# Turning the first half of the heads one hidden tile later in a fused mLSTM and MLP block

## What is computed

```
xn = _layernorm(x, axis=-1)
x = x + _L0_attn_ref(xn, ...) + _L0_ffn_ref(xn, ...)

q = x @ Wq.T; k = x @ Wk.T; v = x @ Wv.T; o_preact = x @ Wog.T
h, state = _mlstm_scan(q, k, v, i_pre, f_pre)
h_norm = _multihead_norm(h, gamma).reshape(B, S, -1)
h_out = jax.nn.sigmoid(o_preact) * h_norm
y = h_out @ Wout.T

gated = jax.nn.silu(gate) * up
return jnp.einsum('bsh,dh->bsd', gated, w_down)
```

## Time and profile before

| | us |
|---|---|
| median of 3 runs | 3110.75 |
| lowest, highest | 3110.28, 3111.6 |
| the profiled execution | 3110.59 |
| its span, first to last instruction | 3108.9 |

### The profile page before, as it was taken

One profiled execution on the slowest core, in us unless ns is written; L12 is line 12 of the kernel. 1 busy time (PEld: TensorE's weight loads), 2 busy tenths in 40 slices (PEclk: granted clock), 3 DMA queues, 4 the chain that ended last, 5 costly groups with the idle time before them and its releaser, 6 DMA issues.

```text
span 3108.9 us, 62468 instructions
## 1 busy us (share of the span) xinstructions
PE 3047.3 (98%) x22090; PEld 2194.9 (71%) x22090; DVE 2347.1 (75%) x5913; ACT 1113.4 (36%) x2160; POOL 781.7 (25%) x1121
## 2 busy tenths in 40 slices
PE   4999999999999999999999999999999999999999
PEld 2677777777777777777777777777777777777776
DVE  7877777777777777777777777777777777777777
ACT  6333333333323333333333333333233333333332
POOL 4222222222222222222222222222222222222222
PEclk9999999999999999999999999999999999999999
DMA  5000000000000000000000000000000000000000
GB/s 224 8 14 13 13 7 7 13 13 13 13 0 13 13 13 13 7 7 13 13 13 13 7 7 13 13 13 13 0 13 13 13 13 7 7 13 13 13 13 7
DMA packets 20334, 51.09 MB, mean 16 GB/s; under 512 B 1506, under 2 KB 1634, under 8 KB 18274
## 3 DMA queue, kind: packets, MB, share of 16 engines
q1 hardware_dynamic: 20322, 50.95, 4.4%
HBM read 34.16 MB, written 16.78 MB: 16 GB/s over the span
## 4 chain that ended last, share of the span: by engine, by line
issue 73%; POOL 22%; PE 2%; DVE 1%; POOLq 1%; ACT 1%; DMA 0%; SPq 0%; DVEq 0%; ACTq 0%
POOL arena L555 9%; POOL pair_r L545 4%; POOL small L574 3%; POOL arena L565 2%; POOL begun L562 1%; POOL small L462 1%; DVE amax L757 1%; PE work L1154 0%; POOLq L554 0%; DMA arena<-w_v_dram 0%; POOL small L464 0%; POOL small L467 0%; POOL small L460 0%; PE work L1119 0%; ACT weights L611 0%
## 5 line engine op out<-in xcount | busy, mean ns | idle before, releaser
L1117 PE MATMUL work<-xt,weights 128*128 128x256 f16 x4608 | 1256.0, 273 | 0.0
L1119 PE MATMUL work<-xt,weights 128*128 128x256 f16 x4608 | 1256.0, 273 | 0.0
L1118 PE MATMUL work<-xt,weights 128*128 128x256 f16 x4608 | 1255.9, 273 | 0.0
L555 POOL TENSOR_TENSOR arena<-arena 128x256 f16<-128x256 f32 x512 | 359.5, 702 | 1628.2 <-ACT arena L689 1628.2
L689 ACT ACTIVATE arena<-arena 128x256 f16<-128x256 f32 x512 | 213.3, 417 | 1057.8 <-DVE arena L983 1057.8
L1117 PEld LDWEIGHTS work<-xt,weights 128*128 128x128 f16 x4608 | 478.5, 104 | 69.2
L1118 PEld LDWEIGHTS work<-xt,weights 128*128 128x128 f16 x4608 | 450.9, 98 | 69.7
L1119 PEld LDWEIGHTS work<-xt,weights 128*128 128x128 f16 x4608 | 450.8, 98 | 52.3
L1117 PE MATMUL acc<-weights,arena 128*128 128x512 f16 x1024 | 388.1, 379 | 0.5 <-POOL arena L555 0.5
L1118 PE MATMUL acc<-weights,arena 128*128 128x512 f16 x1024 | 388.1, 379 | 0.0
L1119 PE MATMUL acc<-weights,arena 128*128 128x512 f16 x1024 | 388.1, 379 | 0.0
(11 more groups left out here) (212 smaller groups left out, 4150.7 us busy)
## 6 DMA issues: line engine op xcount, KB each, us to landing
arena<-x_dram SPq DMA_DIRECT2D x33, 512.0 KB, 3.4
out_dram<-arena SPq DMA_DIRECT2D x32, 512.0 KB, 2.8
weights<-w_g_dram SPq DMA_DIRECT2D x4, 1024.0 KB, 13.2
weights<-w_u_dram SPq DMA_DIRECT2D x4, 1024.0 KB, 20.4
arena<-w_d_dram SPq DMA_DIRECT2D x4, 1024.0 KB, 27.2
arena<-w_qk_dram SPq DMA_DIRECT2D x1, 1024.0 KB, 6.3
arena<-w_v_dram SPq DMA_DIRECT2D x1, 1024.0 KB, 8.3
weights<-w_o_dram SPq DMA_DIRECT2D x1, 1024.0 KB, 25.4
```

Source lines behind the costliest of these rows:

```text
L555: g.tensor_tensor(hh[:, j % HB, 1, :], tt[:, j % 2, :], hh[:, j % HB, 0, :], ALU.subtract).then_inc(h_ready, 1)
L1117: t.matmul(dst, w[0], a[0], start=first, stop=False, skip_group_check=True)
L1118: t.matmul(dst, w[0], a[1], start=False, stop=False, skip_group_check=True)
L1119: return t.matmul(dst, w[1], a[0], start=False, stop=last, skip_group_check=True)
```

## The change

In the table AFTER, hoT0 moves from behind tile 11 to behind tile 12, ahead of the other steps there. In USES it changes places with ffn12, to keep the table in PE's order. Since banks go by place, ffn12 now has bank 2 and hoT0 bank 0; all other uses keep their bank.

```diff
 USES = (["gates", "q", "k", "v0", "v1", "ffn0", "ffn1", "ffn2", "ffn3", "wT", "ffn4", "wbc", "ffn5", "o0",
-         "ffn6", "st0", "ffn7", "ffn8", "st1", "ffn9", "ffn10", "st2", "ffn11", "hoT0", "ffn12", "st3", "o1",
+         "ffn6", "st0", "ffn7", "ffn8", "st1", "ffn9", "ffn10", "st2", "ffn11", "ffn12", "hoT0", "st3", "o1",
          "ffn13", "att0", "ffn14", "ffn15", "hoT1", "att1"])
...
-AFTER[11] = ["hoT0", "turn12", "turn13"]
-AFTER[12] = ["pv3", "o1", "center1"]
+AFTER[11] = ["turn12", "turn13"]
+AFTER[12] = ["hoT0", "pv3", "o1", "center1"]
```

## The result

The changed kernel takes 3129.01 us (median, 3127.39 to 3129.73), the kernel before 3111.1 us (3110.28 to 3111.6); the ratio is 1.0057, with a 95% interval of 1.0042 to 1.0072. It is 18 us slower (17.9 between the medians).

What follows compares the result with a forecast made beforehand. PE, busy 98% of the span, was taken as the bound. Removing the 0.42 us wait and adding one of about 1.0 makes o1 0.57 us later a block: 32 x 0.57 = 18.2 on 3110.75 gives 3129 us, range 3123 to 3136.

Steps and rivals of the forecast that it cites:

- The old wait and its price: At hoT0, PE's transposes wait for DVE's line 1078 of heads0, costing 0.42 us a block between starts.
- The new wait: At o1, PE waits 1.02 us for DVE's line 983 to free tile 12's bank, behind eight transposes.
- The delay from DVE's end to PE's start: At o1, PE starts 0.05 us after DVE frees the bank; 0.15 as the other end.
- Sum: Over the loop, 32 x 0.57 = 18.2 us on top of 3110.75, giving 3129.0 us.
- No second wait behind it: Behind o1, tile 13 has 0.98 us of room and att0 finds hoT0's low part ready, so neither waits.
- Transposes and POOL: On DVE behind tile 11's pair, eight transposes beside POOL's line 555 go free, taking 2.65 us.
- The rival of a held transpose: POOL holds DVE's transposes behind tile 11's pair: 0.42 us a block on top, 0.99 in all, 3142 us; chance 0.06.
- the fourth rival: o1 doesn't wait because DVE frees tile 12's bank 1.02 us earlier: 15.1 us won, 3096 us; chance 0.05.
- the 1093.89 given: Latest end of tile 12's last matmul on PE, placed before the transposes (0.44 us) and down(10) (1.30 us).

Runs made afterwards that it cites:

- the first experiment: Changed kernel with turn12 and turn13 moved from behind tile 11 to behind center1 (tile 12) and scale1 (tile 13): 3095.86 us, ratio 0.9953.

## Why the prediction was right

- **The old wait and its price.** Said: 0.42 us a block between starts, set by heads0. The changed kernel has tile 12 right behind down(9), and with nothing else in the way (the first experiment) a block falls from 94.49 to 94.05 us: 0.44, against the 0.45 worked out.
- **The new wait.** Said: o1 waits for tile 12's line 983, behind eight transposes. Shown by the view of waits, and by the runs with none and with half of the transposes. The wait between starts is 1.43 - 0.45 (the distance without a wait, in the first experiment) = 0.98 us in the block shown, where 1.02 was worked out; the blocks of the two kernels differ by 95.07 - 94.05 = 1.02. Line 983 started 3.58 behind the same line of tile 11 (1096.63 to 1100.21), as the sum 0.45 + 3.13 had it.
- **The delay from DVE's end to PE's start.** I took 0.05 from a row ahead of the loop and kept 0.15 as the other end. Measured: 0.06.
- **Sum.** 0.57 a block was forecast, 0.58 measured; 3129.0 against 3129.01. The hundredths are luck: the runs spread over 2.3 us, and the kernel before came out at 3111.1 and not at the 3110.75 that the sum started from.
- **No second wait behind it.** Right: ACT's copy for the heads and line 1084 come in the places worked out, tile 13 and att0 don't wait.
- **Transposes and POOL.** Line 555 runs beside them (1097.58) and the eight take 2.64. The rival of a held transpose is out. DVE instructions with two inputs in SBUF did take longer beside POOL's in the run with turn11 moved.
- **What was wrong.** One remark in the fourth rival, that transposes ahead of tile 11's pair would free the bank in time. That run gave 3160. The slip was to follow DVE's queue alone, without ACT's, in which the tanh of tile 12 stands behind the copy of tile 11. A slip without effect: between tile 12's last matmul and o1 PE also has pv3, 0.9 us (1098.81 to 1099.26 and 0.45 to the next), so tile 12's matmuls end earlier than the 1093.89 given, and the tanh was no limit all the more.
- **What was not seen.** I gave the exchange of banks no part in the gain: with the old bank tile 12 would have waited for st2, drained behind heads0. It had no part in the forecast time, since the change does both. Nor did I see that the old wait may be in part POOL's: line 1078, which ends it, takes 0.95 us beside line 555 and 0.69 without it.

## What to carry to other kernels

When a step is moved past a use of a shared buffer, list for every later use which use it now follows, and place that one's release through the queues of all engines that it passes. Here the step that was waited for had moved out of the way, and the next user of its bank had inherited a neighbour with eight transposes in front. A freed bank is a threshold: four transposes cost nothing and eight cost 33 us, so look for the slack (0.87 us with none of the transposes, 0.34 with four) before moving anything into it. And look at the place to which a step is moved: turn13 behind heads1 cost 0.22 us a block, which the view of PE's waits doesn't list and only the distances between starts show.

## What the runs showed of the hardware that was not expected

- Behind a wait of about 2.24 us of PE, once a block in an otherwise dense stream, TensorE's clock fell to 1.2 GHz for some eight matmuls of 512 columns in 16 of 31 blocks and in none of the others, though the waits were alike; each time cost 1.69 us. Behind waits of 1.5 us, and of 1.85 us with the old banks, it never fell, nor behind the longer wait that the first block has in each run (2.22 us with two more transposes, 2.92 with four). So the length of the wait doesn't settle it alone.
- At o1 of the changed kernel PE starts 0.06 us after the DVE instruction that frees the bank ends, in all 32 blocks.
- Moving four transposes from in front of heads0, and eight more behind it, made the kernel 17.7 us slower. Some 10 us of it (0.32 a block) are heads0, where DVE's instructions came to lie beside POOL's (0.16 became 0.62 and 0.69 became 1.22), and some 7 (0.22 a block) the last down, put off by the transposes in their new place.
